# Edge counts in ranges of five targets with one tile of edges, instead of eight targets with two

## The reference

```python
# layer 0: attention with 4 heads
proj = (x @ W_proj).reshape(n, 4, 32)
score = leaky_relu(src_score[src] + tgt_score[dst], 0.2)
score = exp(score - max(score))
att = score / (segment_sum(score, dst)[dst] + 1e-16)
out = segment_sum(proj[src] * att, dst)
# layer 1: sum of neighbours, divided by their number, then two products and a layer norm
agg = segment_sum((x @ W_msg.T)[src], dst) / max(deg, 1)
```

## Time and profile before

| what | value |
|---|---|
| median of 3 runs | 4263.77 us (4249.45 to 4268.48) |
| profiled execution, its time | 4262.54 us |
| profiled execution, its span | 4260.7 us |
| busy: PE / DVE / ACT / POOL | 60% / 55% / 23% / 69% of the span |
| mean granted TensorE clock | 0.642 of full speed |
| DMA | 598 MB, 140 GB/s over the span |

### The profile page before, as it was taken

One profiled execution on the slowest core, in us unless ns is written; L12 is line 12 of the kernel. 1 busy time (PEld: TensorE's weight loads), 2 busy tenths in 40 slices (PEclk: granted clock), 3 DMA queues, 4 the chain that ended last, 5 costly groups with the idle time before them and its releaser, 6 DMA issues. The chain is left out here.

```text
span 4260.7 us, 68450 instructions
## 1 busy us (share of the span) xinstructions
PE 2536.6 (60%) x18061; PEld 2185.6 (51%) x18061; DVE 2362.6 (55%) x6832; ACT 983.3 (23%) x2806; POOL 2939.1 (69%) x3036
## 2 busy tenths in 40 slices
PE   2466676665764776744999996767733333333330
PEld 2444454444444666634999996666623333333330
DVE  5577787787874344434666668877722222222224
ACT  0133333333330111112444440111111111111112
POOL 2777666666646777753777777777547777777775
PEclk7566666666656888865555557767866555655565
DMA  4334334333333556635666668878735455444453
GB/s 118 81 93 124 102 106 121 104 107 117 104 92 102 133 135 132 139 49 132 181 176 181 183 163 267 261 245 256 253 88 133 127 133 133 130 132 133 128 133 93
DMA packets 453283, 598.35 MB, mean 140 GB/s; under 512 B 112874, under 2 KB 320830, under 8 KB 450078
## 3 DMA queue, kind: packets, MB, share of 16 engines
q1 hardware_dynamic: 342386, 385.66, 29.8%
q0 software_dynamic: 96672, 200.47, 21.5%
q10 hardware_dynamic: 14000, 9.82, 0.7%
HBM read 419.22 MB, written 180.95 MB: 141 GB/s over the span
## 5 line engine op out<-in xcount | busy, mean ns | idle before, releaser
L613 POOL DMA_INDIRECT G<-table,IC x2128 | 2035.1, 956 | 856.4 <-issue 644.2
L3308 DVE TENSOR_TENSOR_SCAN GW<-BIG,GW,PS 128x512 f32<-128x512 bf16 x208 | 266.3, 1280 | 780.0 <-PE PS L3283 776.3
L3283 PE MATMUL PS<-IDENT,G 128*128 128x128 f32 x832 | 204.6, 427 | 679.8 <-DMA G<-table,IC 679.8
L2902 POOL DMA_INDIRECT G<-table,IC x448 | 465.4, 1039 | 198.6 <-issue 138.9
L3283 PEld LDWEIGHTS PS<-IDENT,G 128*128 128x128 f32 x832 | 163.2, 223 | 716.1 <-DMA G<-table,IC 520.6
L2902 POOL DMA_INDIRECT G<-table2c,IC x384 | 370.8, 966 | 123.0 <-issue 116.5
L1253 PE MATMUL PS<-SEL,GW 128*128 128x96 f32 x1664 | 367.0, 411 | 71.0 <-DVEq L1327 71.0
L1253 PEld LDWEIGHTS PS<-SEL,GW 128*128 128x128 f32 x1664 | 342.6, 314 | 123.0 <-DVEq L1327 123.0
L2916 PE MATMUL PS<-BIG 128*128 128x49 f32 x1680 | 377.5, 412 | 1.1 <-ACT BIG L2851 1.1
L2916 PEld LDWEIGHTS PS<-BIG 128*128 128x128 f32 x1680 | 371.3, 333 | 1.2 <-ACT BIG L2851 1.2
L646 DVE TENSOR_TENSOR SEL<-PS,REL 128x768 f32<-128x768 f32 x266 | 253.1, 951 | 34.6 <-issue 30.4
(11 more groups left out here) (375 smaller groups left out, 4618.8 us busy)
## 6 DMA issues: line engine op xcount, KB each, us to landing
rows_ahead<-G SPq DMA_DIRECT2D x104, 520.0 KB
running_max<-BIG SPq DMA_DIRECT2D x105, 512.0 KB
G<-table,IC POOLq DMA_INDIRECT x2576, 2.6
GW<-source_in_block SPq DMA_DIRECT2D x160, 256.0 KB
SCRATCH<-rows_ahead SPq DMA_DIRECT2D x78, 520.0 KB
SCRATCH<-edge_places SPq DMA_DIRECT2D x209, 192.0 KB
edge_counts<-BIG SPq DMA_DIRECT2D x22, 1568.0 KB
BIG<-run_mask SPq DMA_DIRECT2D x104, 256.0 KB
```

The costliest lines, as they stand in the source:

```text
L613: pool.indirect_dma_start(out=G[:, b, u, 0:width], out_offset=None, in_=table, in_offset=bass.IndirectOffsetOnAxis(ap=IC[:, b * U + u:b * ...
L2902: pool.indirect_dma_start(out=GS[:, b, u, 0:width], out_offset=None, in_=table, in_offset=bass.IndirectOffsetOnAxis(ap=IC[:, b * U + u:b * ...
L3283: last = t.transpose(PS[2 * q + u // 4][:, (u % 4) * P:(u % 4 + 1) * P], G[:, b, u, 0:D], IDENT[:])
L3308: v.tensor_tensor_scan(RM[:, q, h * 512:(h + 1) * 512], MB[:, q, h * 512:(h + 1) * 512], PS[2 * q + h][:], before, ALU.min, ALU.max).then_ ...
```

## The change

A range has 5 targets and one tile of 128 edges. A block of 128 targets is two halves of 64 with 13 ranges each (the last with 4 targets), so 26 ranges, 26 tiles. Ranges go in pairs that share a bank and a one-hot buffer: seven pairs a half (the seventh single). Even groups of a turn take pairs (0, 1) and (2), odd groups (3, 4) and (5, 6). One copy of ACT takes a pair. HOTK has 245 columns (5 x 49), laid out at a pitch of 246. The lists are five columns of ranges with 128 entries (129 for targets) instead of three with 256 (257); so there are five row fetches and ten list fetches. The iotas move to `edge_lists`; the start of a range and of the next one now come through ten small products on PE. In `table0` the row is computed ahead of chunk 5 and the start ahead of chunk 14; six of the list fetches come before POOL's reduction and four behind it, and the wait for them moves to `unpack`. In every group ACT writes the first part of the weights with a second exponential, and the last subtraction of DVE writes the third part itself, so the split takes three operations of DVE instead of five.

```diff
-WN = 8
-WPB = P // WN
+WN = 5
+HALFB = P // 2
+WPH = -(-HALFB // WN)
+WPB = 2 * WPH
+UPB = 2 * (-(-WPH // 2))
...
-        HOTK = LIST[:, at:at + 2 * SPAN].bitcast(BF).rearrange("p (q t c) -> p q t c", q=2, t=2)
-        at += 2 * SPAN
+        HOTK = LIST[:, at:at + 2 * (SPAN + 1)].bitcast(BF).rearrange("p (q t c) -> p q t c", q=2, t=2)[:, :, :, 0:SPAN]
+        at += 2 * (SPAN + 1)
...
-        SPANS = LIST[:, at:at + SPAN // 2].bitcast(BF)
-        at += SPAN // 2
+        SPANS = LIST[:, at:at + (SPAN + 1) // 2].bitcast(BF)[:, 0:SPAN]
+        at += (SPAN + 1) // 2
...
@@ edge_lists, POOL
                     g.drain().then_inc(iotas, 1)
+                    g.iota(THR, [[HALFB, LH], [WN, WPH]], base=0, channel_multiplier=0, allow_small_or_imprecise_dtypes=True)
...
+                    g.drain().then_inc(list_iota, 1)
...
@@ table0, PE
+                            for i in range(LB3):
+                                for k in range(2):
+                                    last = t.matmul(PS[5][:, 8 + 8 * k + i:9 + 8 * k + i], THR[0:1, i * P + k:(i + 1) * P + k],
+                                                    ONE[0:1, 0:1], start=True, stop=True)
...
@@ table0, POOL
                     pool.wait_ge(list_starts, 1)
...
+                    fetch_lists(pool, range(3))
                     pool.wait_ge(red_in, 1)
                     g.partition_all_reduce(SC[:, 8:12], SC[:, 0:4], P, RMAX).then_inc(red_out, 1)
-                    pool.wait_ge(list_in, 32 * LB3)
+                    fetch_lists(pool, range(3, LB3))
...
@@ table0, DVE
-                        if c == 6:
+                        if c == 5:
...
-                        if c == 11:
+                        if c == 14:
...
@@ edges0
+            UNITS = (((0, 1), (2,)), ((3, 4), (5, 6)))
...
             def make_hot(dve, d, b, js):
-                keys = dve.snap(d * (2 * WPB) + b * 8, min_val=0, max_val=2 * DWIN - 8)
+                keys = dve.snap(d * WPB + b // 2 * WPH, min_val=0, max_val=DWIN - WPH)
                 for j in js:
-                    q = j % 2
-                    dve.wait_ge(counted, window_number(d, b, j) + 1)
-                    for tile in range(2):
+                    q = parity(b, j)
+                    dve.wait_ge(counted, pair_number(d, b, j) + 1)
+                    for w in members(j):
...
             def count(pe, d, b, js):
...
-                        last = t.matmul(PS[3 + 4 * q][:, 0:SPAN], HOTL[:, q, tile, :], HOTK[:, q, tile, :],
-                                        start=tile == 0, stop=tile == 1)
+                        last = t.matmul(PS[3 + 4 * q][:, w * SPAN:(w + 1) * SPAN], HOTL[:, q, w, :], HOTK[:, q, w, :],
+                                        start=True, stop=True)
...
             def keep_counts(act, d, s, b, js):
...
+                        a.copy(STAGE[:, s, :, at:at + nodes].rearrange("p h (w n) -> p w h n", w=2),
+                               PS[3 + 4 * q][:, 0:2 * SPAN].rearrange("p (w h n) -> p w h n", w=2, n=WN)).then_inc(kept_counts, 1)
...
                 def act_group(act, pss, turn, b, d=None, s=0):
...
                     act.wait_ge(pe_done, i + 1)
+                    a.activation(WE3[:, q, :, 1:1 + H], ZL[:, q], ACT.Exp, bias=NSHIFT0[:]).then_inc(first_part, 1)
                     a.copy(SELB[:, q], SEL[:, q]).then_inc(copied, 1)
...
                 def dve_group(dve, regs, pss, turn, b, d=None):
...
-                    cg.step(v.tensor_copy(part(0), WEP[:, q]))
+                    dve.wait_ge(first_part, i + 1)
                     cg.step(v.tensor_tensor(Z[:], WEP[:, q], part(0), ALU.subtract))
                     cg.step(v.tensor_copy(part(1), Z[:]))
-                    cg.step(v.tensor_tensor(Z[:], Z[:], part(1), ALU.subtract))
-                    cg.step(v.tensor_copy(part(2), Z[:]))
+                    cg.step(v.tensor_tensor(part(2), Z[:], part(1), ALU.subtract))
```

More of the change, by code:

```diff
@@ L197, in build @@
         NODEW = sb("NODEW", [P, LB3])
+        NEXTW = sb("NEXTW", [P, LB3])
         STARTF = sb("STARTF", [P, LB3])
@@ L471, in table0, with fetch_lists @@
             chunks = [(c, c * 3, min(NB, c * 3 + 3)) for c in range(-(-NB // 3))]
+            def fetch_lists(pool, columns):
+                for i in columns:
+                    pool.indirect_dma_start(
+                        out=DSTI[:, i, :], out_offset=None, in_=DSTP.unsqueeze(1),
+                        in_offset=bass.IndirectOffsetOnAxis(ap=NEXTI[:, i:i + 1], axis=0)).then_inc(list_in, 16)
+                    pool.indirect_dma_start(
+                        out=SRCI[:, i, :], out_offset=None, in_=SRCP.unsqueeze(1),
+                        in_offset=bass.IndirectOffsetOnAxis(ap=STARTI[:, i:i + 1], axis=0)).then_inc(list_in, 16)
             quarters = {3: (0, 12), 7: (12, 24), 11: (24, 36), len(chunks) - 1: (36, NB)}
@@ L522, in _ @@
                     pool.wait_ge(list_starts, 1)
[L523 to L528, removed]
-                            in_offset=bass.IndirectOffsetOnAxis(ap=STARTI[:, i:i + 1], axis=0)).then_inc(list_in, 16)
+                    fetch_lists(pool, range(3))
                     pool.wait_ge(red_in, 1)
                     g.partition_all_reduce(SC[:, 8:12], SC[:, 0:4], P, RMAX).then_inc(red_out, 1)
-                    pool.wait_ge(list_in, 32 * LB3)
+                    fetch_lists(pool, range(3, LB3))
                 @block.vector
@@ L1064, in edges0, with pair_number, parity, members @@
             counts_out, keys_ready, keys_turned = sem("e0_countsout"), sem("e0_keys"), sem("e0_kturned")
-            keys_kept, key_chain = sem("e0_kkept"), sem("e0_kchain")
+            keys_kept, key_chain, first_part = sem("e0_kkept"), sem("e0_kchain"), sem("e0_part0")
             S = Node(sem, "e0")
-            KEY, LOWF, HIF, MORE = (lists(i, 2 * P) for i in range(1, 5))
-            HII, LOWI = (lists(i, 2 * P).bitcast(I32) for i in range(5, 7))
-            LAST_TURN = FIRST + DB
-            def window_number(d, b, j):
-                return d * WPB + b * 4 + j
+            KEY, LOWF, HIF, MORE = (lists(i) for i in range(1, 5))
+            HII, LOWI = (lists(i).bitcast(I32) for i in range(5, 7))
+            UNITS = (((0, 1), (2,)), ((3, 4), (5, 6)))
+            def pair_number(d, b, j):
+                return d * UPB + b // 2 * (UPB // 2) + j
+            def parity(b, j):
+                return (b // 2 * (UPB // 2) + j) % 2
+            def members(j):
+                return range(min(2, WPH - 2 * j))
             def unpack(dve):
                 ck = Chain(dve, key_chain)
+                dve.wait_ge(list_in, 32 * LB3)
                 v.tensor_scalar(HII, SRCI, 7, None, ALU.logical_shift_right)
```

115 lines of the change are left out of this document (58 added, 57 removed).

## The result

The changed kernel takes **4140.93 us** (median of 4, 4135.78 to 4149.02) where the kernel before takes 4264.0 (median of 4): ratio 0.9719, 95% interval 0.969 to 0.9747. The profiled execution took 4138.51 us.

What follows compares the result with a forecast made beforehand. DVE was taken to bound the counted turns, 90.6 us a lap against POOL's 81.0. DVE's 108 us saving, capped at 105, less 7 for the join gives 98; `table0` costs 1: -97, so 4167 us, range 4146 to 4208.

Steps and rivals of the forecast that it cites:

- A: Main forecast: one-hots of 245 columns keep the present slope, POOL's 90.3 us of waits are won; near 4167 us, chance 0.64.
- B: Rival: the odd run of 245 columns loses half its rate, costing 36 us on DVE; 4193 us, chance 0.13.
- C: Rival: HOTK alone falls to 1.0 ns a column, 105 us, eating all gain; 4262 us, chance 0.06.
- D: Rival: HOTK and HOTL both fall to 1.0 ns a column, making the kernel slower; 4310 us, chance 0.05.
- E: Rival: half the gain is lost as DVE finds gathers late after jumps or waits for `first_part`; 4200 us, chance 0.11.
- the join of the two streams: DVE and POOL in `edges0`: the jump-back hole is made good only in part; 7 us lost (0 to 25).
- The gather's pace: POOL in `edges0`: one gather without waits takes 1.266 us, so a lap of 64 takes 81.0 us.
- `table0`: Stage `table0`: moved iotas save, longer search and list fetches cost; net 1 us worse (7.9 better to 7 worse).
- The holes stay in my sum: DVE at the loop's jump back: both holes remain, since a lap's code is smaller by an eighth at most.
- the split: Weights on DVE: two of five steps go, 0.45 us, less 0.1 new wait; net 0.35 x 92 groups, 32 us.
- The tail: End of `edges0`, behind the last gather: 7 us instead of 21.6 if POOL bounds, so 14.6 us gained.
- the cap with all of `table0`'s gain: Lower range end: 105 us (POOL's 90.3 of waits plus 14.6) and 8 for `table0`, about 4151, less some noise.

Runs made afterwards that it cites:

- Ranges alone: The changed kernel with the weights split in five operations again, no second exponential, 240 dead memsets: 4163.01 us, ratio 0.9763; 0.9941 where the kernel before took 5596 to 5688.
- split alone: The kernel before with only the three-operation split, second exponential and 16 dead memsets: 4211.35 against 4265.57 us, ratio 0.9878; 0.9945 where the base took 5596 to 5688.

## Why the prediction was right, and where it was wrong

**Right in mechanism and sign.** A became true: the pair costs 0.36, POOL's waits vanish, DVE begins to wait for gathers. B, C and D fall with the pair's pitch. E falls with POOL's 0.3 us. ACT's wider copies (0.705 us) and second exponential (0.319) are hidden, as charged. DVE's busy time in the counted turns fell by 108 us, the figure of the sum, which is closer than its terms deserve (below).

**Wrong by 26 us of 97, and out of the range by 5.** What failed is the size of four terms, all forecast too dear: the join of the two streams (7 us, measured none), the gather's pace (8 us), `table0` (2 us) and the other stages (nothing was charged, and they came out 10 us shorter). That is 27 us, and the two profiles do differ by 124 where 97 were forecast; the medians differ by 123. The terms:

- "Two streams of equal mean don't run at that mean", 7 us for the join. Nothing was lost: POOL waited 0.3 us. The premise failed, for the streams are not equal. Ranges alone has a lap of 81.4; less eight times 0.50 for the split, DVE would need about 77.4 a lap and POOL 80.2. (An estimate; the changed kernel's 80.2 less its 24.4 us of waits for gathers over ten laps gives 77.7.)
- That DVE came out 3.6 us a lap shorter than the 81.0 forecast has two causes. "The holes stay in my sum" was wrong for the second: I asked whether the lap's code fits, and should have asked how far the next block stands behind the loop's start. That is 3.0 us a lap. And the split was undersized: from the scaling's start to the next one-hot the mean over 84 groups falls from 3.00 to 2.51 us (split alone), 0.50 a group and not 0.35; the 0.1 for the new wait was not there. That makes 1.2 us a lap. Against these 4.2 stand two small ones: the lap before was 90.9 and not 90.6 (21 turns hold ten jumps, not ten and a half), and what else went, beside split and hole, was 6.5 and not 6.8. Since POOL bounds, these 3.6 us a lap show only in the missing join and in the tail.
- The gather's pace of 1.266 us was 0.010 too slow, 8 us over 832. Gathers on POOL take 952 ns in the mean instead of 963, and 64 of them 80.2 to 80.6 us in the counted laps; in the earlier trace rows slower gathers stand among them. The subtraction hid more. Each of the 36 waits in the earlier trace rows holds the 0.3 us that stand ahead of any gather, so POOL waited 79 us and not 90, and its pace without them was 1.279; in the sum the two errors cancel. Why the gathers of the kernel before are slower is open, so this term stays unexplained. With the 7 of the join these are 15 us, and the stage beat its forecast of 98 by 14.
- The tail came out right by luck of a difference. It was read as 21.6 us behind the last gather's end, with a floor of 7; counted to the last row of DVE it was 24.7, and the floor that the changed kernel reached is 10.3. Both were 3 short: 14.6 charged, 14.4 measured.
- `table0`: 1 us worse was forecast, 1.2 better came. The 7.9 us of the earlier trace rows were read as the price of iotas. The iotas take 1.2 us of them; most was POOL's change of configuration, and DVE compares 8.5 us earlier without it. A second change, hidden behind DVE in the kernel before, would have shown behind the longer search; it went too. "I take 3 of the 7.9" was therefore the most undersized term: without both, the changed kernel's stage is 17.3 us shorter (60.1 to 42.8). The price of the longer search was undersized as well: with the iotas in place, the second change now in the open and four fetches behind the reduction, it takes 60.1 where the old one took 44.0. The two errors nearly cancelled.
- Other stages were charged with nothing and are 10 us shorter. In the five profiles of experiments in the short condition they take 2989.8 to 2997.1 us against 2986.0 and 2996.1, so this is mostly scatter; `edges2v_wide` is 3 us of it (5.0 to 2.0) and changes with dead instructions too (4.3 in ranges alone).

The lower end of the range was "the cap with all of `table0`'s gain": it took the pace for exact and left a few microseconds for scatter, where the profiles scatter by 10.

## What to carry to other kernels

Where two engines run side by side, work out both laps as the change leaves them, and take the longer; whatever the shorter one gains beyond that is worth only the lag that it would otherwise pay at the end of the loop (here 11 of 48 us). A hole behind a jump back can be a matter of where the loop lies in the code: before costing it, count the records from the branch to the hole, and see whether dead instructions ahead of the loop move it. Look in POOL's records for reconfigurations before moving an iota or a reduction: what matters is how often the kinds alternate and whether something hides the change, not how long they take.

## What the runs showed of the hardware that was not expected

- A change of POOL's configuration between iotas and the reduction over partitions takes 6.7 to 7.0 us each time and is busy time of nothing; two of them in a stage of 43 us, with what they delay, made 17 us.
- Dead code of 13 or 100 instructions in DVE's program brings a hole of 1 to 4 us a lap or takes it away (seen in the long condition; what it is worth there lies between nothing and 22 us).
- The same program took 4251 to 4266 us or 5596 to 5688 us, not by the chip alone (one of them showed both at different times). The second condition stretches the stages unequally (`edge_lists` hardly, 49.0 to 49.3, `edges0` 1171 to 1513, `layer2` 1171 to 1864, `edges3` 1055 to 1242 us for the kernel before) and halves what a change is worth (0.985 for 0.972). A ratio is told beside the time of its own base.
